# A column scan on TensorE: two of nine passes folded into others, gate biases carried by the weights

## The reference

```
x    = concat(state shifted down, state, state shifted up)   # 96 channels, rows h-1, h, h+1
i    = x @ weight_ih.T + bias_ih                             # r, z, n parts, 32 each
g    = column @ weight_hh.T + bias_hh
r, z = sigmoid(r_i + r_h), sigmoid(z_i + z_h)
n    = tanh(n_i + r * n_h)
state = n * z + column * (1 - z)
```

## Time and profile before

| | |
|---|---|
| time, three runs | median 680.45 us (679.02 to 680.67) |
| profiled execution | 681.49 us, its span 679.7 us |
| busy in the span | PE 613.1, PEld 532.3, ACT 494.9, DVE 486.0, POOL 215.3 us |
| chain that ended last, by line | L576 13%, L573 12%, L562 12%, L538 8% |
| the scan's three PE groups | 756 records each, 105.7 to 110.9 us busy each |
| granted TensorE clock | 0.977 mean |

### The profile page before, as it was taken

The page is one execution under the profiler, slowest core; times in us unless marked ns, Lnnn a source line. Parts: engine busy times, 40 slices in busy tenths (PEclk is TensorE's granted clock), DMA queues, the critical chain, the costliest instruction groups (busy, mean ns, idle before and its releaser), DMA issues.

```text
span 679.7 us, 18532 instructions
## 1 busy us (share of the span) xinstructions
PE 613.1 (90%) x6608; PEld 532.3 (78%) x6608; DVE 486.0 (72%) x1275; ACT 494.9 (73%) x1059; POOL 215.3 (32%) x250
## 2 busy tenths in 40 slices
PE   4689879799999999999999999998778777799996
PEld 2223223499999999999999989998757666699996
DVE  5477684556666666666666668889889989957776
ACT  2345667878888888888888897787739997774442
POOL 6464645012222222222222222203286553302200
PEclk9799898989999999999999999999999998899999
DMA  7700000000000000000000030000215655302215
GB/s 255 283 1 0 1 0 1 1 1 0 0 0 0 0 0 0 0 0 0 0 0 0 0 126 1 1 0 1 88 39 189 217 192 178 124 1 122 110 78 186
DMA packets 10975, 37.35 MB, mean 55 GB/s; under 512 B 2992, under 2 KB 5296, under 8 KB 10048
## 3 DMA queue, kind: packets, MB, share of 16 engines
q1 hardware_dynamic: 9856, 36.71, 15.3%
q10 hardware_dynamic: 672, 0.15, 0.1%
q0 software_dynamic: 416, 0.07, 0.1%
HBM read 28.53 MB, written 8.39 MB: 54 GB/s over the span
## 4 chain that ended last, share of the span: by engine, by line
PE 70%; DVE 16%; ACT 6%; issue 5%; POOL 2%; DVEq 1%; ACTq 0%; POOLq 0%
PE psum L576 13%; PE psum L573 12%; PE psum L562 12%; PE psum L538 8%; DVE work L311 6%; PE psum L648 5%; PE psum L786 4%; PE psum L802 4%; PE psum L664 3%; ACT work L316 2%; PE psum L775 2%; PE psum L632 2%; DVE small L1103 2%; PE psum L706 1%; DVE spec L335 1%
## 5 line engine op out<-in xcount | busy, mean ns | idle before, releaser
L443 POOL TENSOR_TENSOR image<-image,spec 128x128 f32 x128 | 70.9, 554 | 209.1 <-DVE spec L1220 192.7
L576 PE MATMUL psum<-spec,matrices 128*128 128x128 f32 x756 | 110.9, 283 | 1.4 <-ACT spec L885 1.4
L538 PE MATMUL psum<-spec,matrices 128*64 128x512 f32 x384 | 94.6, 651 | 15.2 <-ACT spec L827 7.5
L573 PE MATMUL psum<-spec,matrices 128*128 128x128 f32 x756 | 105.8, 276 | 1.9 <-DVE spec L1200 1.9
L562 PE MATMUL psum<-work,matrices 128*128 (+1 forms) x756 | 105.7, 276 | 0.0
L706 PE MATMUL psum<-work 128*32 128x128 f32 x2368 | 75.1, 282 | 24.8 <-ACT work L316 23.3
L573 PEld LDWEIGHTS psum<-spec,matrices 128*128 128x128 f32 x756 | 95.2, 193 | 2.0 <-DVE spec L1200 2.0
L576 PEld LDWEIGHTS psum<-spec,matrices 128*128 128x128 f32 x756 | 95.1, 193 | 1.7 <-ACT spec L885 1.7
L562 PEld LDWEIGHTS psum<-work,matrices 128*128 128x128 f32 x756 | 95.2, 193 | 0.0
L706 PEld LDWEIGHTS psum<-work 128*32 128x32 f32 x2368 | 66.0, 113 | 33.7 <-issue 28.4
L538 PEld LDWEIGHTS psum<-spec,matrices 128*64 128x64 f32 x384 | 30.0, 148 | 73.3 <-issue 66.1
(11 more groups left out here) (138 smaller groups left out, 981.3 us busy)
## 6 DMA issues: line engine op xcount, KB each, us to landing
work<-w_dram SPq DMA_DIRECT2D x33, 512.0 KB, 3.4
image<-x_dram SPq DMA_DIRECT2D x3, 2048.0 KB, 11.6
out_dram<-image SPq DMA_DIRECT2D x3, 2048.0 KB, 6.3
image<-x_dram SPq DMA_DIRECT2D x4, 512.0 KB, 5.9
work<-w_dram SPq DMA_DIRECT2D x1, 2048.0 KB, 8.1
out_dram<-image SPq DMA_DIRECT2D x4, 512.0 KB, 2.9
kept<-const_dram SPq DMA_DIRECT2D x1, 192.0 KB, 9.7
matrices<-const_dram SPq DMA_DIRECT2D x1, 132.0 KB, 5.9
```

Of the source, the lines that this page charges most:

```text
L443: nc.gpsimd.tensor_tensor(col, col, state[h].unsqueeze(2), ALU.add).then_inc(added[h], 1)
L538: last_mm = mm(psum[o, n % 4, :], cv[:, kx, o], rows_[:, 8 * half:8 * half + 8, kx:kx + W], start=kx == 0, stop=kx == 2)
L573: mm(psum[:, 4 * h + g, 0:HB], sv[:, g, :], state[h], start=g == 2, stop=False)
L576: mm(psum[:, 4 * h + g, 0:HB], sv[:, 3 + g, :], sedge[h], start=False, stop=True).then_inc(s[h], 1)
```

## The change

1. The n-gate's column weight keeps a pass of its own (`sv[:, 6]`), alone left in `from_column`. The r and z column passes go.
2. The edge operand of a half is now two operands, each full: `upper` holds the column in partitions 0 to 63, ones in 64 to 95, the edge from phase 3 in 96 to 127; `lower` holds the edge from phase 0 in 0 to 31, ones in 32 to 63, the column in 64 to 127. Each makes 64 of the 128 outputs: an edge pass is now a pair of matmuls with 128x64 weight tiles, for each of r, n and z. For r and z their weights hold the column's weights, too.
3. There are two such buffers per half (parity of w). SyncE copies the columns into them by DMA inside SBUF, 64 partitions of 512 bytes each, two DMAs for a half step, two steps ahead, when `z_sum` of the step that read the buffer has come. TensorE waits for them (`cur_in`) before the edge passes.
4. The biases of r, z and n_i are put as rows of the edge weights under the ones: VectorE spreads them on diagonals, TensorE turns them with the identity (6 matmuls ahead of the last convolution group), ScalarE copies them into the weights (2 copies). Sigmoid and tanh then take no bias operand. The bias of n_h stays on VectorE.
5. `banks_free` waits for `reset_done` alone.

```diff
-        sedge = [scan_buf() for _ in range(2)]
...
+        upper_e = spec[:, off:off + 4 * HB]
+        lower_e = spec[:, off + 4 * HB:off + 8 * HB]
+        off += 8 * HB
...
+        def edges_of(h, parity):
+            at_ = (2 * h + parity) * HB
+            return upper_e[:, at_:at_ + HB], lower_e[:, at_:at_ + HB]
...
+        bias_z = spec[:, off:off + 3 * C]
...
-                sp.dma_start(sv[C * hi:C * hi + C, 6:9, C * hi:C * hi + C], scan_wh).then_inc(scan_w_in, 16)
-            sp.dma_start(sv[0:C, 3:6, 0:C], scan_wi[:, :, 2 * C:3 * C]).then_inc(scan_w_in, 16)
-            sp.dma_start(sv[C:2 * C, 3:6, P - C:P], scan_wi[:, :, 0:C]).then_inc(scan_w_in, 16)
+                sp.dma_start(sv[C * hi:C * hi + C, 3:5, C * hi:C * hi + C], scan_wh[:, 0:2]).then_inc(scan_w_in, 16)
+                sp.dma_start(sv[C * hi:C * hi + C, 6, C * hi:C * hi + C], scan_wh[:, 2]).then_inc(scan_w_in, 16)
+            sp.dma_start(sv[P - C:P, 3:6, 0:C], scan_wi[:, :, 2 * C:3 * C]).then_inc(scan_w_in, 16)
+            sp.dma_start(sv[0:C, 3:6, P - C:P], scan_wi[:, :, 0:C]).then_inc(scan_w_in, 16)
...
+            def current(h, w, parity):
...
+                up, lo = edges_of(h, parity)
+                for to, q in ((up, slice(0, P // 2)), (lo, slice(P // 2, P))):
+                    sp.dma_start(to[q], columns[q, ds(w * (2 * HB) + h * HB, HB)]).then_inc(cur_in[h][parity], 16)
...
+            sp.wait_ge(columns_ready, B // 2)
+            current(0, 1, 1)
+            current(0, 2, 0)
+            sp.wait_ge(columns_ready, B)
+            sp.wait_ge(last_columns, 1)
+            current(1, 1, 1)
+            current(1, 2, 0)
+            with sp.Fori(0, (W - 4) // 2) as i:
+                for k in range(2):
+                    for h in range(2):
+                        sp.wait_ge(z_sum[h], i * 2 + (k + 1))
+                        current(h, i * 2 + (k + 3), (k + 1) % 2)
+            for h in range(2):
+                sp.wait_ge(z_sum[h], W - 3)
+                current(h, W - 1, 1)
...
+            pe.wait_ge(const_in, 32)
+            pe.wait_ge(bias_spread, 3)
+            for g in range(3):
+                for row in (C, 2 * C):
+                    last = mm(psum[row:row + C, 5, P * g:P * g + P], bias_z[:, C * g:C * g + C], cm["ident"],
+                              start=True, stop=True)
+            last.then_inc(bias_turned, 1)
...
-                for g, bank in ((0, 0), (1, 1), (2, 3)):
-                    mm(psum[:, 4 * h + bank, 0:HB], sv[:, 6 + g, :], columns[:, ds(w * (2 * HB) + h * HB, HB)],
-                       start=True, stop=bank == 3)
+                mm(psum[:, 4 * h + 3, 0:HB], sv[:, 6, :], columns[:, ds(w * (2 * HB) + h * HB, HB)],
+                   start=True, stop=True)
...
-                pe.wait_ge(r_gate[h], w - 1)
-                pe.wait_ge(z_gate[h], w - 1)
...
-            def from_state(h, w):
+            def from_state(h, w, parity, nth):
...
-                    mm(psum[:, 4 * h + g, 0:HB], sv[:, g, :], state[h], start=g == 2, stop=False)
+                    mm(psum[:, 4 * h + g, 0:HB], sv[:, g, :], state[h], start=True, stop=False)
+                pe.wait_ge(cur_in[h][parity], nth * 32)
...
-                    mm(psum[:, 4 * h + g, 0:HB], sv[:, 3 + g, :], sedge[h], start=False, stop=True).then_inc(s[h], 1)
...
+                    for i, e in enumerate(edges_of(h, parity)):
+                        o = slice(i * (P // 2), (i + 1) * (P // 2))
+                        last = mm(psum[o, 4 * h + g, 0:HB], sv[:, 3 + g, o], e, start=False, stop=True)
+                    last.then_inc(s[h], 1)
...
+            pe.wait_ge(bias_written, 2)
...
+            from_state(0, 1, 1, 1)
...
+            from_state(1, 1, 1, 1)
...
-            def scan_step(w):
-                from_state(0, w)
+            def scan_step(w, parity, nth):
+                from_state(0, w, parity, nth)
...
-                from_state(1, w)
+                from_state(1, w, parity, nth)
...
-                    scan_step(i * 4 + (k + 2))
...
+                    scan_step(i * 4 + (k + 2), k % 2, i * 2 + (1 + (k + 1) // 2))
...
+            act.wait_ge(scan_zeroed, 1)
+            act.wait_ge(bias_turned, 1)
+            sv = scan_m[:, :].rearrange("p (k m) -> p k m", m=P)
+            turned = psum[:, 5, 0:3 * P].rearrange("p (k m) -> p k m", m=P)
+            for row, o in ((C, slice(P // 2, P)), (2 * C, slice(0, P // 2))):
+                a(sv[row:row + C, 3:6, o], turned[row:row + C, :, o], ACT.Copy).then_inc(bias_written, 1)
...
-            def state_edges(h, w):
+            def state_edges(h, w, parity):
...
-                e = sedge[h].rearrange("p (b h) -> p b h", h=H4)
-                a(e[0:C, :, 1:H4], s[P - C:P, :, 0:H4 - 1], ACT.Copy).then_inc(sedge_ready[h], 1)
-                a(e[C:2 * C, :, 0:H4 - 1], s[0:C, :, 1:H4], ACT.Copy).then_inc(sedge_ready[h], 1)
+                up, lo = [e.rearrange("p (b h) -> p b h", h=H4) for e in edges_of(h, parity)]
+                a(up[P - C:P, :, 1:H4], s[P - C:P, :, 0:H4 - 1], ACT.Copy).then_inc(sedge_ready[h], 1)
+                a(lo[0:C, :, 0:H4 - 1], s[0:C, :, 1:H4], ACT.Copy).then_inc(sedge_ready[h], 1)
...
-                a(gr[h], psum[:, 4 * h, 0:HB], ACT.Sigmoid, bias=bias_rz[:, 0:1]).then_inc(r_gate[h], 1)
+                a(gr[h], psum[:, 4 * h, 0:HB], ACT.Sigmoid).then_inc(r_gate[h], 1)
...
-                a(gz[h], psum[:, 4 * h + 1, 0:HB], ACT.Sigmoid, bias=bias_rz[:, 1:2]).then_inc(z_gate[h], 1)
+                a(gz[h], psum[:, 4 * h + 1, 0:HB], ACT.Sigmoid).then_inc(z_gate[h], 1)
...
-                a(gn[h], pre2[h], ACT.Tanh, bias=bias_s[:, 2:3]).then_inc(n_gate[h], 1)
...
-            act.wait_ge(bias_ready, 1)
...
-            def scan_step(w):
+                a(gn[h], pre2[h], ACT.Tanh).then_inc(n_gate[h], 1)
...
+            def scan_step(w, parity):
...
-                state_edges(1, w - 1)
+                state_edges(1, w - 1, parity)
...
-                state_edges(0, w)
+                state_edges(0, w, 1 - parity)
...
-                    scan_step(i * 4 + k)
+                    scan_step(i * 4 + k, k % 2)
...
-                v.memset(sedge[i], 0.0).then_inc(pads_zeroed, 1)
+                v.memset(upper_e[96 * i:96 + 32 * i], 1.0 - i).then_inc(pads_zeroed, 1)
+                v.memset(lower_e[C * i:C * i + C], float(i)).then_inc(pads_zeroed, 1)
...
+            dve.wait_ge(small_in, 16 * 8)
+            v.memset(bias_z, 0.0).then_inc(bias_spread, 1)
+            dve.wait_ge(bias_spread, 1)
+            v.tensor_copy(bias_z[:, 0:3 * C:C + 1], bias_s[:, 0:3]).then_inc(bias_spread, 1)
+            v.tensor_copy(bias_z[:, 3:3 + C + 2:C + 1], bias_s[:, 3:5]).then_inc(bias_spread, 1)
...
```

More of the change, by code:

```diff
@@ L132, in program @@
         bias_s = sm(6)
-        bias_rz = sm(2)
         PADW = W + 2
@@ L190, in program @@
         columns_ready, last_columns = sem("columns_ready"), sem("last_columns")
-        bias_ready = sem("bias_ready")
+        bias_spread, bias_turned, bias_written = map(sem, ("bias_spread", "bias_turned", "bias_written"))
+        cur_in = [[sem(f"cur_in{h}{parity}") for parity in range(2)] for h in range(2)]
         state_ready = [sem(f"state_ready{h}") for h in range(2)]
@@ L370, in _ @@
                              scan_wi[:, :, C * (lo - hi + 1):C * (up - hi + 1)]).then_inc(scan_w_in, 16)
-                sp.dma_start(sv[C * hi:C * hi + C, 6:9, C * hi:C * hi + C], scan_wh).then_inc(scan_w_in, 16)
-            sp.dma_start(sv[0:C, 3:6, 0:C], scan_wi[:, :, 2 * C:3 * C]).then_inc(scan_w_in, 16)
-            sp.dma_start(sv[C:2 * C, 3:6, P - C:P], scan_wi[:, :, 0:C]).then_inc(scan_w_in, 16)
+                sp.dma_start(sv[C * hi:C * hi + C, 3:5, C * hi:C * hi + C], scan_wh[:, 0:2]).then_inc(scan_w_in, 16)
+                sp.dma_start(sv[C * hi:C * hi + C, 6, C * hi:C * hi + C], scan_wh[:, 2]).then_inc(scan_w_in, 16)
+            sp.dma_start(sv[P - C:P, 3:6, 0:C], scan_wi[:, :, 2 * C:3 * C]).then_inc(scan_w_in, 16)
+            sp.dma_start(sv[0:C, 3:6, P - C:P], scan_wi[:, :, 0:C]).then_inc(scan_w_in, 16)
             sp.dma_start(kept[:, :], const_d[:, 0:sum(KEPT_COLS.values())]).then_inc(const_in, 16)
             sp.dma_start(forward_m, const_d[:, sum(KEPT_COLS.values()):]).then_inc(const_in, 16)
+            def current(h, w, parity):
+                up, lo = edges_of(h, parity)
+                for to, q in ((up, slice(0, P // 2)), (lo, slice(P // 2, P))):
+                    sp.dma_start(to[q], columns[q, ds(w * (2 * HB) + h * HB, HB)]).then_inc(cur_in[h][parity], 16)
+            sp.wait_ge(pads_zeroed, 12)
+            sp.wait_ge(columns_ready, B // 2)
[13 more added lines that the diff above has]
+                current(h, W - 1, 1)
             sp.wait_ge(state_ready[0], W)
@@ L430, in _ @@
             pool.wait_ge(scan_zeroed, 1)
-            pool.wait_ge(pads_zeroed, 10)
+            pool.wait_ge(pads_zeroed, 12)
             for u in range(GB):
@@ L545, in _ @@
             sum0_of(0, 1, steps_mean(1))
```

(46 more changed lines are left out.)

1 line of the change is left out of this document (removed).

## The result

| | before | changed |
|---|---|---|
| median of 4 runs, us | 680.11 | 668.71 (667.33 to 671.00) |
| ratio to before | | 0.9834, interval 0.9809 to 0.9860 |
| profiled execution, span | 681.49, 679.7 | 671.00, 669.2 |
| ScalarE, TensorE loads busy in the span | 494.9, 532.3 | 450.0, 479.9 |

11.4 us less (9.5 to 13.0 by the interval); 15 were forecast, and the time lies in the range. The period of a half step, averaged over the last 118 periods of sigmoid z, went from 2.047 to 1.950 us; over 125 periods that is 12 us, so the scan holds all of it. (From the last sigmoid to the end of the span it is 285.3 us before, 287.5 in the changed kernel's profile and 285.2 when it was profiled again; over all twelve profiles of this document it lies between 285.2 and 288.0, so no change of 2 us could be told there.)

What follows compares the result with a forecast made beforehand. A ScalarE-TensorE loop of 2.05 us per half step was the bound, TensorE close behind. It becomes 0.94 + 0.30 + 0.69 = 1.93; 125 periods give 15 us less, 665.5 us; own range 659 to 672, with rivals 659 to 682.

Steps and rivals of the forecast that it cites:

- A loop of ScalarE and TensorE ends last, TensorE 0.05 behind: Scan half step: edge load, sigmoid z, two copies, next edge load take 2.05 us; TensorE's 18 records take 1.98.
- Bias operand, 0.093 us: Sigmoid z in the loop: without its bias operand 0.093 us shorter, so 0.39 becomes 0.30; bounds 0 and 0.10.
- Pairs side by side, first one 0.05 us late: Edge passes: a 128x64 pair costs a full record's 0.11 us; edge load to sigmoid z 0.94 for 0.97.
- Rival 4: ScalarE-TensorE loop: bias saving doesn't come or pairs start slowly; loop 2.02 or 2.00, 675 us; chance 0.07.
- Two changes of width, 0.34 us: TensorE in each half step: tile width changes twice, drains and uncovered loads add 0.34 us; TensorE 1.88.
- rival 2: Width changes: next load waits for the last matmul's full end (0.28), T = 2.04, 680 us, no change; chance 0.12.
- Rival 1: TensorE was the bound and width changes cost nothing: T = 1.54, 64 us less, 617 us; chance 0.05.
- The columns' DMAs, 0: SyncE's feed: two issues 0.8 to 1.5 us, data wanted 6.8 us later; hidden, 0.
- rival 3: TensorE's wait for cur_in: fed columns land late (7.1 us), period 2.15, 693 us; chance 0.09.
- The state's way round, 1.88: Scan, edge load to edge load of the same half through the state: T + 1.88 = 2T, T = 1.88 us.
- Before the scan, 0: Start: first column, diagonals, small copies, memsets and fewer early records sum to 0, bounds -0.5 and +2.5 us.
- rival 5: Granted clock falls as TensorE is no longer always busy: streams of 0.21, over 750 us; chance 0.03.

Runs made afterwards that it cites:

- e1: Kernel before, nine passes, sigmoid r, sigmoid z and tanh without bias operand, biases of r, z and n_i left out; 675.64 us, 0.9915 of before.
- e7: Kernel before with the edge passes in the order r, z, n instead of r, n, z; 673.93 us, 0.9909 of before.
- e2: Changed kernel, seven passes, with a bias operand (a tile of zeros) given back to the three activations; 680.92 us, 1.0004 of before.
- e3: Kernel before, nine passes, only its three edge passes issued as pairs of 128x64 weight tiles; 718.82 us, 1.0554 of before.
- e6: Against e5: state passes and n_h's column pass also as pairs, order r, z, n_h, n, no change of width in the scan; 648.35 us, 0.9520 of before.
- e5: Changed kernel with the edge passes in the order r, z, n instead of r, n, z; 662.96 us, 0.9738 of before.
- e4: Changed kernel with TensorE's wait for the fed column moved ahead of its wait for the state; 666.62 us, 0.9798 of before.
- e8: Against e6: TensorE's wait for the fed column moved ahead of its wait for the state; 649.53 us, 0.9548 of before.
- e9: Against e8: ScalarE does the other half's two edge copies between sigmoid r and sigmoid z; 662.30 us, 0.9725 of before.

## Why the prediction was right, and what it missed

- *A loop of ScalarE and TensorE ends last, TensorE 0.05 behind.* Right. e1 and e7 shorten the loop in two different ways, by 0.09 and by 0.18, and both stop at 2.010 with TensorE's loads end to end; e2 removes two passes and changes next to nothing (2.038). The gap was 0.037.
- *Bias operand, 0.093 us.* Sigmoid z took 278 ns after 367, 0.089 less. In the loop sigmoid to copy went from 0.39 to 0.30. e2 takes just this away again and loses all the gain.
- *Pairs side by side, first one 0.05 us late.* Edge load to sigmoid z 0.925 for 0.94, where no wait stands in front of the load. The last term was 0.68 for 0.69. Rival 4 falls.
- *Two changes of width, 0.34 us.* 0.33 in e3. The load starts 0.20 after the last matmul's start also where that has 128 elements (301.40 to 301.60 above), so rival 2 (0.28) falls. The drain that the Trainium skill states (page "TensorEngine Tiling (Array Packing)", section "Key Properties") is shown here with a price in e3 and e6: it kept TensorE at 1.90 and was, in e5, on the path: 14.6 us between e5 and e6. Rival 1 was wrong by this and by the loop.
- *The columns' DMAs, 0.* The data were hidden (1.8 us landing; rival 3 falls); the wait for them was not. This is the term that was mis-sized: the sum gave the added wait no cost, since what it waits for was long there. As a second wait on the matmul that ends the loop it cost 0.08 us in every second half step, 0.04 in the mean, 125 x 0.04 = 5 us. e4 moves it, and its ordinary half steps are 1.905 long. The loop's other terms add up to just that, 0.925 + 0.30 + 0.68, and not to the forecast's 1.93: 3 us to the good. So two errors of opposite sign partly cancelled, and that is luck: 15 - 5 + 3 = 13, against 12 by the periods and 11.4 by the medians (9.5 to 13.0). That e4's mean hits 1.93 is chance as well: its loop is shorter, and VectorE's late start in one half step of six, which the prediction did not have, fills it up.
- *The state's way round, 1.88.* Not on the path in the change: TensorE's state group stands behind line 601's, not behind the state. e8 shows it as the limit, at 1.735 in ordinary half steps. The estimate has 0.20 for the drain where a step without one takes 0.11; without it T is 1.79, so it was 0.05 too high.
- *Before the scan, 0.* The six diagonal matmuls ran from 99.23 in TensorE's wait. The first edge load came at 134.3 for 135.2, and at 133.8 when profiled again; e1 and e7, which have none of the preparation, had 134.5 and 133.1, so no difference shows.
- *Clock.* Granted 1.00 from 150 to 350 us; rival 5 falls.
- *The range.* Its upper end comes out at 673 with the prediction's own terms (665.5 + 125 x 0.04 + 2.5), not 672; nothing hangs on it.

## What to carry to other kernels

In a loop that several engines pass through in turn, take a distance between the same two instructions one period apart and split it at each handover; an engine at 100% busy may be second. When two limits stand close, measure each half of a change alone: here they gave 5.5 and 0 us, together 11.4. Look at the single periods, not only at their mean: a mean that hits the forecast can be a shorter loop and a rare long step. Put an added wait on an instruction that has slack, not on the one that closes the loop, even if what it waits for is always there; and before folding passes into narrower tiles, either make all passes in the loop the same width or price the drain.

## What the runs showed of the hardware that was not expected

- In the changed kernel, a second wait in front of a weight load, for something that was long there, cost 0.06 us in front of the load (0.11 after the copy's end for 0.05) and 0.02 behind it.
- VectorE's first operation in each iteration of its program loop started 0.30 after its operation before, in e8, the others up to 0.08 before that one's end. Kernels with slack hid it; the fastest ones paid 0.05 us a half step for it.
- Activations behind one another start before the other ends in some places: tanh 0.21 us after the start of a copy of 0.30 (300.44 and 300.65 above), sigmoid z 0.20 after one in e9 (291.75 and 291.95). A copy behind a copy started 0.32 after it, in none of the twelve profiles earlier. Before the change tanh started 0.03 after the copy's end (303.32 by the line below, 303.35 in the earlier trace rows), and in e1, without its bias operand, 0.02 after. What decides it was not tried.
```profile
303.02 0.30 ACT L885 ACTIVATE spec<-spec 32x120 f32<-32x120 f32 x1
```
